# Attention and feed-forward stack: scores in two halves, products in two parts, and the variance by one full matmul

## The chip, the cores and the metric

The kernel runs on one core of one Trainium2 chip. The metric is the device time of one execution in microseconds (us), the median of several runs. The core has five engines that run side by side and meet only at semaphores: TensorE (PE: matmuls out of SBUF into PSUM), VectorE (DVE), ScalarE (ACT), GpSimd (POOL, which here touches SBUF alone) and SyncE (SP, which here issues the transfers).

## What is computed

The input is 2 batches of 1024 tokens of 128 features. The program is: norm and a first small attention, norm and a stack of six layers, norm and a second small attention, norm and the same stack again. Only the stack (`_L0_ffn_ref`) is touched. Cut to what matters, in fp32:

```python
for i in range(6):                        # 16 heads of 64, windows of 32
    x = attn_layer(shift_tokens(x), Wqkv[i], ...) + x
    x = ffn_layer(shift_tokens(x), ...) + x

def attn_layer(x, Wqkv, qs, ksc, Wo):
    q, k, v = split(x @ Wqkv)             # 128 -> 3 * 1024
    q, k = l2norm(q) * qs, l2norm(k) * ksc   # per head, then rotary tables
    out = local_attention(q, k, v)        # each window of 32 looks at itself and the one before
    return out @ Wo                       # 1024 -> 128

def ffn_layer(x, g, bln, W1, b1, W2, b2):
    mu = x.mean(-1); var = ((x - mu) ** 2).mean(-1)
    xn = (x - mu) / sqrt(var + 1e-05) * g + bln
    a, gate = split(xn @ W1 + b1)         # 128 -> 2 * 341
    return a * gelu(gate) @ W2 + b2
```

## The kernel before

`ffn_stack` is called twice, and each call runs 6 layers of 16 tiles of 128 tokens: 96 tiles. It is a software pipeline written out by hand. Each engine has a loop over the same slots `s`, 96 with a tile of their own (`live(s)`) and 13 more that drain. In slot `s` TensorE projects q, k and v of tile `s`, transposes the rotated and normalised q and k of tile `s-1` and forms its scores, forms the products of attention weights and v for tile `s-2` (`values`), and projects the output of tile `s-3` (`out_part`). The feed-forward part works on blocks of four tiles: `feed(s, lag)` names a block only in one slot of four. So slots come in four kinds by `s % 4`, called phase 0 to 3 here:

- phase 3: `feed(s, 7)` centres a block (L1140), squares and averages it, and `feed(s, 11)` does the third piece of the hidden half;
- phase 0: `feed(s, 8)` spreads the inverse deviation (L1145) and scales, and `feed(s, 12)` does the three matmuls with W2 (L1166, L1177, L1190);
- phase 1: `feed(s, 9)`, three gate matmuls (L1117); phase 2: `feed(s, 10)`, two hidden matmuls (L1117).

The order on an engine is the order of its instructions; nothing is scheduled elsewhere. TensorE's order in a slot is: q projection (L1077), q and k transposes (L1213, L1219), k projection, mask and scores (L1085, L1094), v projection, and then four parts of `values` (L1107, 32 matmuls each; an fp32 matmul leaves two records in the trace, so a part shows as 64) with `feed_first`, `feed_second` and `feed_third` between them, `feed_fourth`, and `out_part` (L1131). In phases 2 and 3 the first half of `out_part` stands between the third and the fourth part of `values`. Scores and products use small pieces of the array (64 rows by 32 columns, and 32 rows by 64), the others all of it.

Before `feed_first` TensorE waits for the evacuation of v (L1293 on ACT), since v's PSUM banks 6 and 7 are used again. Before the q projection of the next slot it waits for `o_ev`, the evacuation of the products (L1311 on ACT), which leave banks 0 to 3. Between one slot's projections and the next slot's transposes lies a chain over the other engines: ACT squares q (L1264), DVE rotates q and k (L1401 to L1404), takes the row maximum of the scores (L1440, which needs all scores), subtracts it (L1443), sums the squares (L1410, L1449), ACT takes logarithm and exponential (L1305, L1307), and POOL makes a Newton step (L1351 to L1357) and multiplies q, then k (L1361).

For the variance, TensorE takes each of four tiles of `xsq` as the stationary operand against one column `mean_of` (L1184), DVE adds epsilon (L1465), ACT makes a seed (L1317, L1319), POOL makes four small Newton operations (L1371 to L1377, 128x4), and TensorE spreads the result over the partitions (L1145), which DVE multiplies in (L1472) and POOL shifts (L1380).

## Time and profile before

| | us |
|---|---|
| median of 3 runs (4534.43 to 4556.44) | 4546.21 |
| the profiled execution, its own time | 4545.58 |
| its span, first to last instruction | 4543.7 |
| PE busy / DVE busy | 4139.5 / 3252.4 |
| ACT busy / POOL busy | 2299.8 / 2320.7 |
| mean granted TensorE clock | 0.964 of full speed |

The span is one execution on the chip. The two stacks fill it from about 420 to 2210 us and from about 2710 us to the end. A busy engine counts the durations of its instructions; a TensorE record's duration contains its pipeline's tail, so that records overlap and what counts for TensorE is the distance from one start to the next.

### The profile page before, as it was taken

The numbers are of one execution on the slowest core, as the hardware profiler recorded it, in microseconds if no ns is written. First come the engines' busy times: TensorE is split into PE (matmuls) and PEld (weight loads), VectorE is DVE, ScalarE is ACT, GpSimd is POOL, SyncE is SP. The second block draws the span as 40 slices with busy tenths as digits, with TensorE's granted clock in tenths as the row PEclk, the third lists the DMA queues.
The fourth block names the chain that finished last, engine by engine and source line by source line (L and its number), as shares of the span: only waits on it lengthen the run. The fifth ranks groups of instructions, "written<-read, shape, count | busy, mean of one in ns | idle before, by whom it ended". The sixth has DMA issues, their size and how long they took to land. (4 is left out here: it accounts for less than half of the span.)

```text
span 4543.7 us, 196701 instructions
## 1 busy us (share of the span) xinstructions
PE 4139.5 (91%) x90200; PEld 2525.9 (56%) x90200; DVE 3252.4 (72%) x4377; ACT 2299.8 (51%) x3044; POOL 2320.7 (51%) x2036
## 2 busy tenths in 40 slices
PE   6886899999999999999678877999999999999997
PEld 2322566666666666666333324666666666666664
DVE  7996677777777777777354435677777777777774
ACT  6884445555454555545224443455545455554553
POOL 0001567666666766766100005676676666666662
PEclk8998899999999999999789988999999999999998
DMA  0001111111211111111000001111111111121110
GB/s 19 1 1 40 44 51 39 52 40 45 55 31 54 46 41 53 37 31 31 12 1 1 1 12 55 51 42 50 46 42 52 37 54 46 35 60 37 31 35 20
DMA packets 92032, 162.95 MB, mean 36 GB/s; under 512 B 33996, under 2 KB 55240, under 8 KB 91208
## 3 DMA queue, kind: packets, MB, share of 16 engines
q1 hardware_dynamic: 91208, 150.36, 12.2%
q8 instruction: 712, 11.67, 1.1%
q14 instruction: 112, 0.92, 0.1%
HBM read 48.61 MB, written 1.05 MB: 11 GB/s over the span
## 5 line engine op out<-in xcount | busy, mean ns | idle before, releaser
L1107 PEld LDWEIGHTS banks<-f_P_T,f_V_previous 32*64 32x64 f32 x24576 | 482.6, 131 | 500.8 <-issue 479.9
L1349 POOL TENSOR_TENSOR f_q_rotated<-f_rope_aq,f_rope_bq 128x1024 f32<-128x1024 f32 x192 | 455.7, 2373 | 334.9 <-DVE f_rope_bq L1404 334.3
L1077 PE MATMUL banks<-f_wqkv,H 128*128 128x512 f32 x1152 | 574.5, 623 | 45.3 <-DMA f_wqkv<-in_L_ffn_Wqkv 21.2
L1107 PE MATMUL banks<-f_P_T,f_V 32*64 32x32 f32 x24576 | 577.9, 223 | 34.8 <-issue 33.6
L1401 DVE TENSOR_TENSOR f_rope_aq<-banks,f_rope 128x1024 f32<-128x1024 f32 x192 | 235.1, 1225 | 495.3 <-ACT f_sqq L1264 451.4
L1107 PE MATMUL banks<-f_P_T,f_V_previous 32*64 32x32 f32 x24576 | 569.0, 227 | 21.0 <-issue 13.7
L1349 POOL TENSOR_TENSOR f_k_rotated<-f_rope_ak,f_rope_bk 128x1024 f32<-128x1024 f32 x192 | 451.5, 2352 | 213.4 <-DVE f_rope_bk L1404 213.4
L1077 PE MATMUL banks<-f_wqkv,G 128*128 128x512 f32 x1152 | 554.0, 603 | 0.6
L1107 PEld LDWEIGHTS banks<-f_P_T,f_V 32*64 32x64 f32 x24576 | 441.3, 133 | 39.5 <-issue 38.4
L1336 POOL MEMSET f_kT<- 128x256 f32 x2 | 0.6, 311 | 847.6 <-POOLq L215 847.6
L1131 PE MATMUL banks<-f_O_T,f_wo 128*128 128x128 f32 x3072 | 429.7, 289 | 2.2 <-issue 2.1
L1264 ACT ACTIVATE f_sqq<-banks 128x1024 f32<-128x1024 f32 x192 | 197.0, 1026 | 439.4 <-PE banks L1077 439.4
L1131 PEld LDWEIGHTS banks<-f_O_T,f_wo 128*128 128x128 f32 x3072 | 382.9, 197 | 34.1 <-issue 26.0
L1293 ACT ACTIVATE f_V<-banks 128x1024 f32<-128x1024 f32 x192 | 196.5, 1023 | 401.5 <-PE banks L1077 401.5
L1311 ACT ACTIVATE f_O_T<-banks 128x1024 f32<-128x1024 f32 x192 | 196.5, 1023 | 363.1 <-PE banks L1107 363.0
L1361 POOL TENSOR_TENSOR f_q_rotated<-f_q_rotated,f_inverse_norm 128x1024 f32<-128x1024 f32 x192 | 365.1, 1902 | 15.1
L1367 POOL TENSOR_TENSOR f_E<-f_E,f_row_inverse 128x1024 f32<-128x1024 f32 x192 | 365.4, 1903 | 12.9 <-DVE f_row_inverse L1455 12.9
L1361 POOL TENSOR_TENSOR f_k_rotated<-f_k_rotated,f_inverse_norm 128x1024 f32<-128x1024 f32 x192 | 365.0, 1901 | 0.0
L1117 PE MATMUL banks<-f_xn,f_w 128*128 128x512 f32 (+1 forms) x576 | 322.8, 645 | 33.0 <-ACT f_V L1293 20.7
L1351 POOL TENSOR_TENSOR f_rsqrt_tmp<-f_rsqrt_seed 128x32 f32<-128x32 f32 x192 | 45.7, 238 | 553.3 <-ACT f_rsqrt_seed L1307 553.3
L1077 PEld LDWEIGHTS banks<-f_wqkv,H 128*128 128x128 f32 x1152 | 204.4, 198 | 210.4 <-issue 194.9
L1094 PEld LDWEIGHTS banks<-f_kT,f_qT 64*32 64x32 f32 x24576 | 253.9, 105 | 84.2 <-issue 81.7
(174 smaller groups left out, 8379.8 us busy)
## 6 DMA issues: line engine op xcount, KB each, us to landing
f_V_previous<-f_V SPq DMA_DIRECT2D x192, 384.0 KB, 3.7
f_V_previous<-f_V SPq DMA_DIRECT2D x192, 128.0 KB, 2.3
f_wqkv<-in_L_ffn_Wqkv SPq DMA_DIRECT2D x48, 384.0 KB, 4.0
f_rope<-in_rope SPq DMA_DIRECT2D x24, 512.0 KB, 5.2
f_wo<-in_L_ffn_Wo SPq DMA_DIRECT2D x12, 512.0 KB, 5.4
f_w<-in_L_ffn_W SPq DMA_DIRECT2D x12, 341.0 KB
f_w<-in_L_ffn_W SPq DMA_DIRECT2D x24, 64.0 KB
xin<-in_L_attn_a_x SPq DMA_DIRECT2D x2, 512.0 KB, 5.0
```

Of the source, the lines that this page charges most:

```text
L1077: mm = nc.tensor.matmul(ps[:, o * BLK:(o + 1) * BLK], xs, w[:, c * INNER + o * BLK:c * INNER + (o + 1) * BLK], start=True, stop=True)
L1094: mm = nc.tensor.matmul(PT_S[g * W:(g + 1) * W, c:c + 2 * W], qT[rows, k, g * W:(g + 1) * W], kT[u][rows, k, g * W:(g + 2) * W], start=Fal ...
L1107: mm = nc.tensor.matmul(banks[i * DH:(i + 1) * DH, g * BLK + k * W:g * BLK + (k + 1) * W], of[n % 3][r, h * DH:(h + 1) * DH], PT[n % 2][r, ...
L1117: nc.tensor.matmul(banks[0:k, bk * BLK:(bk + 1) * BLK], w1[b // NBLK % 2][:, half * DI + o:half * DI + o + k], xn[:], start=True, stop=Tru ...
L1131: mm = nc.tensor.matmul(bank(4, P), wo[layer(s - 3) % 2][:, k, :], OT[(n - 3) % 2][:, :, k, :], start=k == 0, stop=k == HP - 1)
L1264: nc.scalar.activation(sq[i][:], ps, ACT.Square).then_inc(sqd.sem, 1)
L1293: nc.scalar.activation(V[n % 3][:], PV_F, ACT.Copy).then_inc(v_ev.sem, 1)
L1311: nc.scalar.activation(OT[n % 2][:].rearrange("p g k t -> p g (k t)"), banks[:, 0:4 * BLK].rearrange("p (g c) -> p g c", g=NG)[:, :, 0:HP ...
L1349: nc.gpsimd.tensor_tensor(qk[i][:], ra[i][:], rb[i][:], ALU.add).then_inc(radd.sem, 1)
L1361: nc.gpsimd.tensor_tensor(heads_of(qk[i][:]), heads_of(qk[i][:]), over(rn[:, i * HEADS:(i + 1) * HEADS], DH), ALU.mult)\
L1367: nc.gpsimd.tensor_tensor(e, e, over(ri[:], DH), ALU.mult).then_inc(pn.sem, 1)
L1401: nc.vector.tensor_tensor(heads_of(ra[i][:]), src, table(2 * i, 0, DH), ALU.mult).then_inc(rot.sem, 1)
```

## The change

- `scores` is called in two halves of 4 head pairs each. The first half of the v projection stands between them, the second half behind them.
- `values` has two parts, of four head pairs (64 matmuls) each, and `out_part` is always whole and last. `feed_first` and `feed_second` stand together between the two parts; the first W2 matmul moves to `feed_first` and the second to `feed_second`.
- The variance is one matmul with a 128x128 stationary operand of 1/128 and `xsq` of 512 columns as the moving one. Its result is the variance of every token already spread over all partitions. So the four matmuls that spread it (L1145) go, and the steps on DVE, ACT and POOL that made it from 128x4 are 128x512 now. They use `xsq` as their temporary, and `rstd` stands in `var`.

```diff
-                    scores(n - 1, (s - 1) % TPB)
+                    scores(n - 1, (s - 1) % TPB, 0, HP // 2)
                 if live(s):
                     pe.wait_ge(kT_ev.sem, kT_ev.past(n - 1))
-                    project(s, 2, PV_F).then_inc(v_mm.sem, 1)
+                    project(s, 2, PV_F, 0, 1)
+                if live(s - 1):
+                    scores(n - 1, (s - 1) % TPB, HP // 2, HP)
+                if live(s):
+                    project(s, 2, PV_F, 1, 2).then_inc(v_mm.sem, 1)
...
-                    values(n - 2, 0, 2)
+                    values(n - 2, 0, 4)
...
                 feed_first(s)
-                if live(s - 2):
-                    values(n - 2, 2, 4)
                 feed_second(s)
                 if live(s - 2):
-                    values(n - 2, 4, 6)
+                    values(n - 2, 4, 8)
                 feed_third(s)
-                if live(s - 3) and s % TB >= 2:
-                    out_part(s, 0, HP // 2)
-                if live(s - 2):
-                    values(n - 2, 6, 8)
                 feed_fourth(s)
                 if live(s - 3):
-                    out_part(s, HP // 2 if s % TB >= 2 else 0, HP)
+                    out_part(s, 0, HP)
...
-                if (b := feed(s, 8)) is not None:
-                    pe.wait_ge(f_nt.sem, f_nt.at(blk(b)))
-                    for t in range(TB):
-                        mm = nc.tensor.matmul(banks[:, 6 * BLK + t * P:6 * BLK + (t + 1) * P],
-                                              rstd[:, t:t + 1].to_broadcast([P, P]), ident[:], start=True, stop=True)
-                    mm.then_inc(f_bc.sem, 1)
...
-                    for t in range(TB):
-                        mm = nc.tensor.matmul(banks[:, 5 * BLK + t:5 * BLK + t + 1], xsq[:, t * P:(t + 1) * P],
-                                              mean_of[:], start=True, stop=True)
-                    mm.then_inc(f_var.sem, 1)
+                    nc.tensor.matmul(bank(5), mean_of[:], xsq[:], start=True, stop=True).then_inc(f_var.sem, 1)
...
-                    nc.scalar.activation(vlg[:], var[:], ACT.Ln).then_inc(f_seed.sem, 1)
+                    nc.scalar.activation(xsq[:], var[:], ACT.Ln).then_inc(f_seed.sem, 1)
...
-                    nc.gpsimd.tensor_tensor(vrt[:], vy0[:], vy0[:], ALU.mult).then_inc(f_nt.sem, 1)
+                    nc.gpsimd.tensor_tensor(xsq[:], vy0[:], vy0[:], ALU.mult).then_inc(f_nt.sem, 1)
...
-                    nc.gpsimd.tensor_tensor(rstd[:], vrt[:], vy0[:], ALU.mult).then_inc(f_nt.sem, 1)
+                    nc.gpsimd.tensor_tensor(var[:], xsq[:], vy0[:], ALU.mult).then_inc(f_nt.sem, 1)
...
-                    nc.vector.scalar_tensor_tensor(xn[:], xcs[:], vec[b // NBLK % 2][:, 0:1], bank(6), ALU.mult, ALU.mult)\
+                    nc.vector.scalar_tensor_tensor(xn[:], xcs[:], vec[b // NBLK % 2][:, 0:1], var[:], ALU.mult, ALU.mult)\
```

How this moves TensorE's instructions, in the middle of a slot (`x64` counts matmuls of the program). Before, the scores stand in one piece and the v projection behind them:

```order
L1085 MATMUL banks<-f_band_mask,ident 128x512 x2
L1094 MATMUL banks<-f_kT,f_qT 32x64 x64
L1077 MATMUL banks<-f_wqkv,G 128x512 x2
L1107 MATMUL banks<-f_P_T,f_V_previous 64x32 x8
```

The same place of the changed kernel, where L1081, L1090, L1072 and L1104 are mask, scores, projection and products:

```order
L1081 MATMUL banks<-f_band_mask,ident 128x512 x2
L1090 MATMUL banks<-f_kT,f_qT 32x64 x32
L1072 MATMUL banks<-f_wqkv,G 128x512
L1090 MATMUL banks<-f_kT,f_qT 32x64 x32
L1072 MATMUL banks<-f_wqkv,G 128x512
L1104 MATMUL banks<-f_P_T,f_V_previous 64x32 x8
```

TensorE enters small pieces twice there now, with one matmul of the v projection between. The second place is the end of a phase 3 slot. Before, part three of the products, half the output projection, part four, the variance and the rest:

```order
L1107 MATMUL banks<-f_P_T,f_V 64x32 x8
L1131 MATMUL banks<-f_O_T,f_wo 128x128 x4
L1107 MATMUL banks<-f_P_T,f_V_previous 64x32 x8
L1107 MATMUL banks<-f_P_T,f_V 64x32 x8
L1107 MATMUL banks<-f_P_T,f_V_previous 64x32 x8
L1107 MATMUL banks<-f_P_T,f_V 64x32 x8
L1184 MATMUL banks<-f_mean_of,f_x_squared 128x1 x4
L1131 MATMUL banks<-f_O_T,f_wo 128x128 x4
L1077 MATMUL banks<-f_wqkv,G 128x512 x2
```

And the changed kernel from the second part's end on (L1174 is the variance, L1128 the output projection):

```order
L1104 MATMUL banks<-f_P_T,f_V 64x32 x8
L1174 MATMUL banks<-f_x_squared,f_mean_of 128x512
L1128 MATMUL banks<-f_O_T,f_wo 128x128 x8
L1072 MATMUL banks<-f_wqkv,G 128x512 x2
```

The output projection is in one piece and stands wholly behind the products. The third place is POOL, between the last multiplication of phase 3 (L1367) and the additions for the next tile (L1349), before:

```order
L1367 TENSOR_TENSOR f_E<-f_E,f_row_inverse 128x1024
L1371 TENSOR_TENSOR f_var_tmp<-f_var_seed 128x4
L1373 TENSOR_TENSOR f_var_tmp<-f_var_tmp,f_var 128x4
L1375 TENSOR_SCALAR f_var_tmp<-f_var_tmp 128x4
L1377 TENSOR_TENSOR f_rstd<-f_var_tmp,f_var_seed 128x4
L1349 TENSOR_TENSOR f_q_rotated<-f_rope_aq,f_rope_bq 128x1024
```

and in the changed kernel:

```order
L1354 TENSOR_TENSOR f_E<-f_E,f_row_inverse 128x1024
L1357 TENSOR_TENSOR f_x_squared<-f_var_seed 128x512
L1359 TENSOR_TENSOR f_x_squared<-f_x_squared,f_var_then_rstd 128x512
L1361 TENSOR_SCALAR f_x_squared<-f_x_squared 128x512
L1363 TENSOR_TENSOR f_var_then_rstd<-f_x_squared,f_var_seed 128x512
L1336 TENSOR_TENSOR f_q_rotated<-f_rope_aq,f_rope_bq 128x1024
```

The order there is the same; the four operations are 128 times as wide.

## Rows read from the trace of the kernel before

**Rows 1.** The page: the span, and TensorE's busy time.

```profile
span 4543.7 us, 196701 instructions
...
PE 4139.5 (91%) x90200; PEld 2525.9 (56%) x90200; DVE 3252.4 (72%) x4377; ACT 2299.8 (51%) x3044; POOL 2320.7 (51%) x2036
```

**Rows 2.** Windows, by engine: busy us (instructions), then PEclk, DMA share, GB/s.

```profile
1005.00:1010.00 5.00, 5.00 (x27) 3.70 (x27) 0.93 (x4) 1.43 (x3) 5.00 (x3) 0.66 0.40 108
...
1400.00:1800.00 400.00, 389.76 (x9827) 254.82 (x9824) 307.28 (x401) 210.75 (x276) 262.69 (x232) 1.00 0.18 48
```

**Rows 3.** Timeline of PE, a phase 2 slot: start, us, instruction, records, [idle before].

```profile
1045.87 1.88 PE L1077 MATMUL banks<-f_wqkv,H 128*128 128x512 f32 x4
...
1048.46 1.04 PE L1219 MATMUL banks<-ident,f_k_rotated 128*128 128x128 f32 x8
...
1051.58 1.48 PE L1094 MATMUL banks<-f_kT,f_qT 64*32 64x64 f32 x128
1052.99 1.98 PE L1077 MATMUL banks<-f_wqkv,H 128*128 128x512 f32 x4
1054.93 0.32 PE L1107 MATMUL banks<-f_P_T,f_V_previous 32*64 32x32 f32 x13
...
1056.09 1.12 PE L1117 MATMUL banks<-f_xn,f_w 128*128 128x512 f32 x2 [0.31 <-ACT f_V L1293]
1057.15 0.34 PE L1107 MATMUL banks<-f_P_T,f_V_previous 32*64 32x32 f32 x16
...
1057.94 1.12 PE L1117 MATMUL banks<-f_xn,f_w 128*128 128x512 f32 x2
...
1062.84 1.98 PE L1077 MATMUL banks<-f_wqkv,H 128*128 128x512 f32 x4
```

**Rows 4.** Timeline of PE, the three slots behind it (phases 3, 0, 1).

```profile
1065.54 1.04 PE L1219 MATMUL banks<-ident,f_k_rotated 128*128 128x128 f32 x8
...
1080.62 1.88 PE L1077 MATMUL banks<-f_wqkv,H 128*128 128x512 f32 x4
...
1096.41 1.12 PE L1190 MATMUL banks<-f_gate,f_w 85*128 85x512 f32 x2
1097.37 1.95 PE L1131 MATMUL banks<-f_O_T,f_wo 128*128 128x128 f32 x16
1099.16 1.88 PE L1077 MATMUL banks<-f_wqkv,H 128*128 128x512 f32 x4
...
1116.77 0.59 PE L1077 MATMUL banks<-f_wqkv,H 128*128 128x512 f32 x1
```

**Rows 5.** Timeline of DVE, ACT and POOL, same slots.

```profile
1054.75 1.22 DVE L1440 TENSOR_REDUCE f_row_max<-banks 128x16 f32<-128x1024 f32 x1
1055.02 1.02 ACT L1293 ACTIVATE f_V<-banks 128x1024 f32<-128x1024 f32 x1
...
1063.43 1.90 POOL L1361 TENSOR_TENSOR f_k_rotated<-f_k_rotated,f_inverse_norm 128x1024 f32<-128x1024 f32 x1
```

**Rows 6.** Groups of instructions: xcount, then busy us, mean ns, idle before.

```profile
L1349 POOL TENSOR_TENSOR f_q_rotated<-f_rope_aq,f_rope_bq 128x1024 f32<-128x1024 f32 x192 | 455.7, 2373 | 334.9 <-DVE f_rope_bq L1404 334.3 <-PE banks L1213 0.6
...
L1332 POOL TENSOR_TENSOR f_rope<-f_rope,f_qk_scales 128x512 f32<-128x512 f32 x48 | 59.6, 1273 | 20.7 <-DMA f_qk_scales<-in_L_ffn_k_scale 20.7
...
L1380 POOL TENSOR_SCALAR f_xn<-f_xn,f_ln_g_ln_b_b 128x512 f32<-128x512 f32 x48 | 33.3, 693 | 4.3 <-DVE f_xn L1472 4.3
...
L1298 ACT ACTIVATE f_x_squared<-banks 128x512 f32<-128x512 f32 x48 | 28.7, 597 | 59.9 <-PE banks L1140 59.9
```

**Rows 7.** Timeline of POOL and DVE around the phase 0 slot.

```profile
1084.23 0.20 POOL L1371 TENSOR_TENSOR f_var_tmp<-f_var_seed 128x4 f32<-128x4 f32 x1
...
1095.04 0.24 POOL L1351 TENSOR_TENSOR f_rsqrt_tmp<-f_rsqrt_seed 128x32 f32<-128x32 f32 x1 [3.02 <-ACT f_rsqrt_seed L1307]
...
1095.77 0.69 DVE L1472 SCALAR_TENSOR_TENSOR f_xn<-f_x_centered,f_ln_g_ln_b_b,banks 128x512 f32<-128x512 f32 x1
```

**Rows 8.** Timeline of POOL in the first stack's drain.

```profile
2201.39 0.20 POOL L1371 TENSOR_TENSOR f_var_tmp<-f_var_seed 128x4 f32<-128x4 f32 x1 [27.57 <-ACT f_var_seed L1319]
```

More of the change, by code:

```diff
@@ L1071, in banks67_free, with project @@
                     pe.wait_ge(h_new.sem, h_new.at(blk(b)))
-            def project(s, c, ps):
+            def project(s, c, ps, o0=0, o1=2):
                 xs = state(s)[:, col(s):col(s) + P]
                 w = wqkv[layer(s) % 2]
-                for o in range(2):
+                for o in range(o0, o1):
                     mm = nc.tensor.matmul(ps[:, o * BLK:(o + 1) * BLK], xs,
@@ L1079, in project, with scores @@
                 return mm
-            def scores(n, t):
+            def scores(n, t, k0, k1):
                 u = n % 2
-                pe.wait_ge(qT_ev.sem, qT_ev.at(n))
-                for i in range(2):
-                    nc.tensor.matmul(PT_S[:, i * BLK:(i + 1) * BLK], ident16[:],
-                                     mask[:, (1 if t else 0):(2 if t else 1), :].to_broadcast([P, HP, 2 * W]),
-                                     start=True, stop=False)
-                pe.wait_ge(kT_ev.sem, kT_ev.at(n))
-                for k in range(HP):
+                if k0 == 0:
+                    pe.wait_ge(qT_ev.sem, qT_ev.at(n))
+                    for i in range(2):
+                        nc.tensor.matmul(PT_S[:, i * BLK:(i + 1) * BLK], ident16[:],
+                                         mask[:, (1 if t else 0):(2 if t else 1), :].to_broadcast([P, HP, 2 * W]),
+                                         start=True, stop=False)
+                    pe.wait_ge(kT_ev.sem, kT_ev.at(n))
+                for k in range(k0, k1):
                     for i in range(2):
@@ L1096, in scores @@
                                 kT[u][rows, k, g * W:(g + 2) * W], start=False, stop=k == HP - 1)
-                mm.then_inc(s_mm.sem, 1)
+                if k1 == HP:
+                    mm.then_inc(s_mm.sem, 1)
             def values(n, k0, k1):
@@ L1141, in feed_first @@
                                      start=True, stop=True).then_inc(f_xc.sem, 1)
-                if (b := feed(s, 8)) is not None:
-                    pe.wait_ge(f_nt.sem, f_nt.at(blk(b)))
-                    for t in range(TB):
-                        mm = nc.tensor.matmul(banks[:, 6 * BLK + t * P:6 * BLK + (t + 1) * P],
-                                              rstd[:, t:t + 1].to_broadcast([P, P]), ident[:], start=True, stop=True)
-                    mm.then_inc(f_bc.sem, 1)
                 if (b := feed(s, 9)) is not None:
@@ L1154, in feed_first @@
                     hidden(b, 0, 0, 6, f_a.sem)
+                if (b := feed(s, 12)) is not None:
+                    pe.wait_ge(f_hm.sem, f_hm.at(blk(b), 2))
+                    nc.tensor.matmul(bank(7), w2[b // NBLK % 2][:, 0, :], ge[:, 0, :], start=True, stop=False)
             def feed_second(s):
@@ L1164, in feed_second @@
                 if (b := feed(s, 12)) is not None:
-                    pe.wait_ge(f_hm.sem, f_hm.at(blk(b), 2))
-                    nc.tensor.matmul(bank(7), w2[b // NBLK % 2][:, 0, :], ge[:, 0, :], start=True, stop=False)
+                    nc.tensor.matmul(bank(7), w2[b // NBLK % 2][:, 1, :], ge[:, 1, :], start=False, stop=False)
             def feed_third(s):
@@ L1175, in feed_third @@
                     hidden(b, 1, 2, 5, f_g.sem)
-                if (b := feed(s, 12)) is not None:
-                    nc.tensor.matmul(bank(7), w2[b // NBLK % 2][:, 1, :], ge[:, 1, :], start=False, stop=False)
             def feed_fourth(s):
@@ L1297, in _ @@
                     act.wait_ge(f_xc.sem, f_xc.at(blk(b)))
+                    act.wait_ge(f_nt.sem, f_nt.past(blk(b) - 1))
                     nc.scalar.activation(xsq[:], bank(6), ACT.Square).then_inc(f_sq.sem, 1)
@@ L1316, in _ @@
                     act.wait_ge(f_nt.sem, f_nt.past(blk(b) - 1))
-                    nc.scalar.activation(vlg[:], var[:], ACT.Ln).then_inc(f_seed.sem, 1)
+                    nc.scalar.activation(xsq[:], var[:], ACT.Ln).then_inc(f_seed.sem, 1)
                     act.wait_ge(f_seed.sem, f_seed.at(blk(b), 1))
-                    nc.scalar.activation(vy0[:], vlg[:], ACT.Exp, scale=-0.5).then_inc(f_seed.sem, 1)
+                    nc.scalar.activation(vy0[:], xsq[:], ACT.Exp, scale=-0.5).then_inc(f_seed.sem, 1)
                 if (b := feed(s, 9)) is not None:
@@ L1464, in _ @@
                     dve.wait_ge(f_nt.sem, f_nt.past(blk(b) - 1))
-                    nc.vector.tensor_scalar(var[:], bank(5, TB), EPS, None, ALU.add).then_inc(f_eps.sem, 1)
+                    nc.vector.tensor_scalar(var[:], bank(5), EPS, None, ALU.add).then_inc(f_eps.sem, 1)
                 if (b := feed(s, 8)) is not None:
```

19 lines of the change are left out of this document (7 added, 12 removed).

## Prediction

> **What bounds the kernel now.** I read the page first: TensorE is busy for 4139.5 of 4543.7 us, DVE, the next, for 3252.4 [rows 1]. Then the windows: from 1400 to 1800 us TensorE has work in 389.76 of 400 us, at the full granted clock, while DVE rests for nearly a quarter [rows 2]. So in the steady stack the length of a slot is the sum of TensorE's distances from start to start, and the timeline gives it. The q projections of five slots start at 1045.87, 1062.84, 1080.62, 1099.16 and 1116.77 [rows 3, 4]: phases 2, 3, 0 and 1 take 16.97, 17.78, 18.54 and 17.61 us, 70.90 for four slots. I call such four a period. All five stand in one place where nothing else disturbed TensorE.
>
> The reader should see one thing inside a slot. Small pieces are cheap and going in and out of them is dear. 128 score records take 1051.58 to 1052.99, 1.41 us; 64 product records take 1057.15 to 1057.94, 0.79 us [rows 3]. Half the records cost more than half the time: 64 more records cost 0.62, and 0.17 us is paid once a stretch. On the other side, two full records between two small parts take 1056.09 to 1057.15, 1.06 us, while a further record of a projection costs only 0.43 (four last 1.88 and one 0.59 [rows 4], so 1.29 for three), 0.86 for two. A stretch of small pieces thus costs 0.17 + 0.20 = 0.37 us beside its records. Second: the first part of the products, 1054.93 to 1056.09, takes 1.16 instead of 0.79, and the row names why: an idle 0.31, ended by the evacuation of v (1055.02 + 1.02 = 1056.04 [rows 5]).
>
> The second limit is near. k is multiplied on POOL until 1063.43 + 1.90 = 1065.33 [rows 5], and its transposes start at 1065.54 [rows 4]: 0.21 us of room, or 0.16 when 0.05 goes for a handoff (1056.04 to 1056.09 above). From one slot's k transposes, 1048.46 [rows 3], the chain over ACT, DVE and POOL needs until 1065.38, 16.92 us. No slot in which that chain is unchanged can be shorter than 16.92.
>
> **The change part by part**, TensorE first, from a slot's q projection.
>
> Up to the scores nothing changes: 1045.87 to 1051.58, 5.71 us. Scores and v projection took 1051.58 to 1054.93, 3.35. They are now two stretches of 64 records with two full records behind each: 0.79 + 1.06 + 0.79 + 1.06 = 3.70, so 0.35 is added in each slot. Products begin at 9.41.
>
> The first part of the products has 128 records, 0.79 + 0.62 = 1.41, taken as 1.44 with 0.01 a record. v's evacuation takes the same 1.16 from the end of the projection as before and is covered now: 0.37 us of waiting goes, and 0.28 of room is left. The feeds then stand together, four full records in phases 0 to 3: 1.06 + 0.86 = 1.92, until 12.77. The first and second W2 matmul are moved into this place in phase 0; both wait for gated values made two slots before, and nothing waits there. The second part is 1.44, until 14.21.
>
> Behind it phases 3, 0 and 1 have two full records (variance, third W2 matmul, third gate matmul) and the 16 of the output projection. The rows have just that: 1096.41 to 1097.37 to 1099.16, 0.96 + 1.79 = 2.75 [rows 4]. These slots end at 16.96. Phase 2 has the output projection alone, 1.79 + 0.10 for entering from small pieces: 16.10. The variance matmul is in these sums. It costs 0.96 in place of eight narrow records, so little moves there; the four spreading matmuls of phase 0 are simply gone.
>
> TensorE's own sum is 3 x 16.96 + 16.10 = 66.98. But 16.10 is under the chain's 16.92, so TensorE will wait some 0.82 us for k at the start of phase 3. The period is 3 x 16.96 + 16.92 = 67.80, which is 3.10 less than 70.90.
>
> Now what the chain sees. Its one new partner on TensorE is the row maximum, which needs all scores: they end at 5.71 + 2.64 = 8.35, and DVE gets to them at 1054.75 - 1045.87 = 8.88 [rows 3, 5]. So there is 0.4 of room and the later scores are free; without that room each 0.1 us would cost 0.1 in all 176 slots with feeds, 18 us. The earlier o_ev is free too: the products leave banks 0 to 3 1.8 us before the q projection, more than ACT's 1.02.
>
> Wider steps: epsilon on DVE and Ln and Exp on ACT go from 0.2 to about 0.6 us each (597 ns for 128x512 on ACT [rows 6]). They stand at the end of phase 3, behind the output's evacuation and ahead of the next squares. DVE is free for epsilon near 16.4, by its work before, and three steps of 0.6 with handoffs end near 18.4; queued behind them on ACT are the squares of the next q, wanted at 16.96 + 1.9 = 18.9. So 0.5 of room hides them.
>
> POOL's Newton step is the large one. 128x512 costs 1273 ns for a tensor_tensor and 693 for a tensor_scalar [rows 6]: 3 x 1.27 + 0.69 + three handoffs of 0.08 = 4.75 us in place of 1.1. No row shows these very operations; the bounds are nothing more than that line at one end and, at the other, the 2373 ns of an operation twice as wide, 8.05 us in all. I take the 1.27, the same width and form. Before, it started 3.61 us into phase 0 (1084.23 - 1080.62); phase 3 ahead of it is 0.82 shorter now and POOL's work is not, so it starts at 4.4 and ends at 9.2. Queued behind it are the two additions of some 2.37 us each: they end at 13.95. POOL's next need is the seeds at 1095.04 - 1080.62 = 14.42 [rows 7]. So 0.45 us of room is left and the step costs nothing while it is there. Without it, each us beyond costs 44 us over the run.
>
> The scaling L1472 reads the deviation from SBUF now, so both its tensors lie there. The row shows 0.69 us at 1095.77 with one of the two from PSUM, at the time of POOL's small Newton operations [rows 7]; no row has two from SBUF beside POOL. Between no cost and the whole 0.69 put in front of POOL's multiplications I take none for the sum. The Trainium skill speaks against that: "SBUF — State Buffer", the section on the separate sides of SBUF, says that a DVE operation with two SBUF inputs and a GpSimd operation take a shared pair of ports as an exclusive lock, and that the loser waits for the whole instruction. By it the sum would be that of the second rival below.
>
> Sum: 96 tiles a call less the first 8 slots, which have no feeds yet, make 22 periods, 44 in two calls: 44 x 3.10 = 136 us. The drain pays for the wider chain, since there everything waits for it: POOL idled 27.57 us before the last Newton step [rows 8]. 3.65 on POOL, 0.8 on ACT, 0.4 on DVE, less 1.1 for the spreading: 3.8 a call, 8 in two. The first 8 slots are bound by the chain and I leave them. 136 - 8 = 128, and 4545.58 - 128 = 4418. The profiled execution stands 0.6 us from the median of the runs, so this is the forecast for both.
>
> **The rivals.**
>
> *TensorE's sum alone* (chance 0.06): k comes earlier than I read, the period is 66.98, 44 x 3.92 = 172, less 8: 4382. Against it stands the 1065.33, which no part of the change moves.
>
> *DVE and POOL hinder each other at the scaling* (0.22). It starts at 15.15 in phase 0, amid small Newton operations that end at 15.6. If POOL's next steps wait some 0.55 us for it, k is ready at 17.47, not 16.92, and the slot is 0.5 longer: 44 x 0.5 = 22, so 4440. If instead DVE waits for both of POOL's multiplications, its additions to the state come 3.7 us late and the next q transposes stall for some 1.7 us: 75 us, so 4493. For it, only what the skill says in the place named above; against it, POOL's even durations, which no such operation ever met. The first form is the likelier.
>
> *POOL's Newton step overruns* (0.06). At 8.05 us it ends 3.3 later, 2.85 past its room; the slot becomes 19.8: 44 x 2.8 = 123, so 4541. A third of that gives 4460. Against: the 1273 ns are a mean of 48 with the same width.
>
> *The clock falls* (0.09), the one that ends on the other side. At 1005 to 1010 the granted clock was 0.66: of these 5 us 0.34 x 2 x 5 = 3.4 ran at 1.2 GHz in place of 2.4, which lost 1.7 [rows 2]. The changed kernel has, in every slot, small scores, two full records and 128 small products, 3.3 us with only 0.86 us of full records, and the wait of 0.8 in phase 3. If that lets the clock fall, each such stretch costs 1.7 us; 75 of them, one in 2.3 slots, cancel the 128, and one in each slot gives 4418 + 176 x 1.7 = 4717. The gain also removes causes: the wait for v and the narrow records. Against it: 1400 to 1800 at full clock with parts much like these.
>
> **How the numbers follow.** Forecast 0.57, its own range 4400 to 4436; the rivals 0.06, 0.22, 0.06, 0.09 as above. About 0.5%, 23 us, is what a measurement of this kernel can tell from no change. Faster by more: all but the worst of the overrun and the half of the clock's case that costs over 100 us, 0.90. The clock's case holds 0.05 for slower and most of the rest is the same. The range 4380 to 4490 takes TensorE's sum alone, both usual forms of the hindrance and a mild overrun: 0.83.
>
> **What would show it.** The period of q projections at 67.8; TensorE idle about 0.8 us before the k transposes in phase 3 alone, released by POOL; no idle before the first feed; 1.41 to 1.44 for 128 product records and 1.06 for half a v projection; POOL's three wide products at 1.27 us and its additions done before the seeds. Wrong would be: waits before the row maximum, k transposes waiting in phase 1 (hindrance) or before phase 1 by over 1 us (overrun), a mean clock under 0.96.

## The result: 0.36% faster, and the profile after

| | us |
|---|---|
| before, median of 20 runs (4534.43 to 4556.44) | 4544.64 |
| changed, median of 20 runs (4515.93 to 4548.97) | 4528.38 |
| ratio, with its 95% interval | 0.9964 (0.9955 to 0.9974) |
| the profiled execution of the changed kernel, its own time | 4523.63 |

The gain is 16 us where 128 were forecast. It is real, but inside the 0.5% that the prediction called no change, and outside its range. The page, which answers to [rows 1], shows that the span fell by 22 us in this execution, and TensorE's busy time by 85:

```profile
span 4521.8 us, 195415 instructions
...
PE 4054.1 (90%) x89528; PEld 2431.3 (54%) x89528; DVE 3279.5 (73%) x4377; ACT 2343.3 (52%) x3044; POOL 2495.5 (55%) x2036
...
q8 instruction: 707, 11.58, 1.1%
```

TensorE was thus idle or slow for most of what it saved. Windows over the two stacks (busy us and instructions of PE, PE's loads, DVE, ACT and POOL, then the granted clock, DMA share, GB/s):

```profile
570.00:2150.00 1580.00, 1515.87 (x38406) 974.21 (x38409) 1227.56 (x1585) 845.57 (x1079) 1131.76 (x924) 0.98 0.16 44
2900.00:4400.00 1500.00, 1441.64 (x36584) 924.01 (x36582) 1172.56 (x1513) 807.20 (x1029) 1080.88 (x882) 0.99 0.16 44
```

The first stretch of the kernel before, for comparison:

```profile
570.00:2150.00 1580.00, 1542.23 (x38621) 1010.06 (x38613) 1211.46 (x1579) 824.81 (x1078) 1050.21 (x922) 1.00 0.16 44
```

Where TensorE idled stands in the waits of the whole execution (us in total, times, longest):

```profile
PE banks L1104 <- issue: 116.6, 148, 2.5
...
PE banks L1128 <- issue: 19.5, 18, 2.4
...
PE banks L1207 <- POOL f_k_rotated L1348: 13.1, 26, 0.8
```

L1104 are the products. "issue" says that nothing in the program held them: no semaphore, no tile. The kernel before had this row too, less than half as large, and a wait for v that is gone now:

```profile
PE banks L1107 <- issue: 47.3, 58, 2.2
...
PE banks L1117 <- ACT f_V L1293: 20.7, 71, 0.3
```

One slot of phase 3, the counterpart of [rows 4], shows the rest. It is the timeline of PE; rows of a run that alternate between the two V tiles are left out:

```profile
1060.33 1.06 PE L1207 MATMUL banks<-ident,f_k_rotated 128*128 128x128 f32 x8 [0.21 <-POOL f_k_rotated L1348]
1061.23 1.88 PE L1072 MATMUL banks<-f_wqkv,H 128*128 128x512 f32 x4
...
1063.47 0.86 PE L1090 MATMUL banks<-f_kT,f_qT 64*32 64x64 f32 x64
1064.26 1.12 PE L1072 MATMUL banks<-f_wqkv,H 128*128 128x512 f32 x2
1065.32 0.86 PE L1090 MATMUL banks<-f_kT,f_qT 64*32 64x64 f32 x64
1066.10 1.12 PE L1072 MATMUL banks<-f_wqkv,H 128*128 128x512 f32 x2
1067.16 0.34 PE L1104 MATMUL banks<-f_P_T,f_V_previous 32*64 32x32 f32 x16
...
1068.30 0.28 PE L1104 MATMUL banks<-f_P_T,f_V 32*64 32x32 f32 x5
1069.36 0.31 PE L1104 MATMUL banks<-f_P_T,f_V 32*64 32x32 f32 x7 [0.78 <-issue]
1069.60 1.13 PE L1137 MATMUL banks<-G,f_center 128*128 128x512 f32 x2
1070.57 1.02 PE L1114 MATMUL banks<-f_xn,f_w 128*85 128x512 f32 x2
1071.52 0.34 PE L1104 MATMUL banks<-f_P_T,f_V_previous 32*64 32x32 f32 x16
...
1072.67 0.59 PE L1104 MATMUL banks<-f_P_T,f_V 32*64 32x32 f32 x13
1073.19 1.12 PE L1174 MATMUL banks<-f_x_squared,f_mean_of 128*128 128x512 f32 x2
1074.15 1.95 PE L1128 MATMUL banks<-f_O_T,f_wo 128*128 128x128 f32 x16
1075.94 1.88 PE L1072 MATMUL banks<-f_wqkv,H 128*128 128x512 f32 x4
```

Read the starts against the prediction. Half scores 0.79, half v projection 1.06, again 0.78 and 1.06: 3.69, as forecast 3.70. The two feeds 1.92, as forecast. Variance and output projection 0.96 + 1.79, as forecast. But the first product run takes 1067.16 to 1069.60, 2.44 us in place of 1.44, and the second 1.67. In the first, five records start from 1068.30 on and the next at 1069.36, a microsecond later: TensorE halts within one and the same run. (The row's 0.78 is counted from the modelled end of the record ahead.) Of the 174 product runs between 570 and 2150 us the shortest takes 1.42, so the 1.44 is possible; the median is 1.66 and the mean 1.80. The same holds for whole slots: the shortest of phases 0 to 3 take 16.89, 16.85, 16.03 and 16.89 us, close to the forecast, but their means are 18.14, 18.05, 17.07 and 18.28.

What ends a halt? The DMA view of this stretch, 1063 to 1074 us in 40 slices of 0.275 us, shows a queue that the prediction never looked at:

```profile
GB/s 0 0 0 0 0 0 0 0 0 0 0 0 0 60 0 0 0 0 0 0 0 0 0 0 0 0 0 60 0 0 0 0 0 0 0 0 0 0 0 0
...
q8 instruction: 2, 0.03, 1.2%
```

### The profile page after: what moved, and what is told of

Same layout as the page of the kernel before. It is cut to its first block and busy times, and to the rows that moved or that the text cites. A ratio compares the mean times of both kernels' runs of the same rounds, so it can differ in the third digit from the quotient of the medians.

```text
span 4521.8 us, 195415 instructions
## 1 busy us (share of the span) xinstructions
PE 4054.1 (90%) x89528; PEld 2431.3 (54%) x89528; DVE 3279.5 (73%) x4377; ACT 2343.3 (52%) x3044; POOL 2495.5 (55%) x2036
## 3 DMA queue, kind: packets, MB, share of 16 engines
q8 instruction: 707, 11.58, 1.1%
## 5 line engine op out<-in xcount | busy, mean ns | idle before, releaser
L1104 PEld LDWEIGHTS banks<-f_P_T,f_V_previous 32*64 32x64 f32 x24576 | 485.8, 131 | 341.8 <-issue 340.4
L1072 PE MATMUL banks<-f_wqkv,H 128*128 128x512 f32 x1152 | 597.2, 629 | 44.6 <-DMA f_wqkv<-in_L_ffn_Wqkv 21.3
L1104 PE MATMUL banks<-f_P_T,f_V 32*64 32x32 f32 x24576 | 555.0, 225 | 73.2 <-issue 72.0
L1104 PE MATMUL banks<-f_P_T,f_V_previous 32*64 32x32 f32 x24576 | 548.2, 227 | 46.7 <-issue 44.6
L1072 PE MATMUL banks<-f_wqkv,G 128*128 128x512 f32 x1152 | 579.8, 612 | 0.0
L1104 PEld LDWEIGHTS banks<-f_P_T,f_V 32*64 32x64 f32 x24576 | 463.2, 132 | 82.2 <-issue 81.0
L1128 PEld LDWEIGHTS banks<-f_O_T,f_wo 128*128 128x128 f32 x3072 | 395.0, 203 | 97.0 <-issue 94.5
L1128 PE MATMUL banks<-f_O_T,f_wo 128*128 128x128 f32 x3072 | 409.2, 289 | 19.7 <-issue 19.5
L1090 PEld LDWEIGHTS banks<-f_kT,f_qT 64*32 64x32 f32 x24576 | 267.1, 105 | 227.2 <-issue 224.6
L1090 PE MATMUL banks<-f_kT,f_qT 64*32 64x64 f32 x24576 | 328.9, 224 | 1.5 <-ACT f_kT L1267 1.5
L1114 PE MATMUL banks<-f_xn,f_w 128*128 128x512 f32 (+1 forms) x576 | 304.8, 640 | 23.1 <-DVE H L1467 11.3
L817 DVE TENSOR_REDUCE soft_neg_max<-banks 128x3 f32<-128x1536 f32 (+11 forms) x219 | 176.5, 854 | 163.1 <-PE banks L710 111.5
```

The lines of the kernel that those rows point to most:

```text
L817: nc.vector.tensor_reduce(pm[r % 2][:, it, jc, h0:h1], strips(j, h0, h1, n), AX.X, ALU.max, negate=True).then_inc(maxed, 1)
L1072: mm = nc.tensor.matmul(ps[:, o * BLK:(o + 1) * BLK], xs, w[:, c * INNER + o * BLK:c * INNER + (o + 1) * BLK], start=True, stop=True)
L1090: mm = nc.tensor.matmul(PT_S[g * W:(g + 1) * W, c:c + 2 * W], qT[rows, k, g * W:(g + 1) * W], kT[u][rows, k, g * W:(g + 2) * W], start=Fal ...
L1104: mm = nc.tensor.matmul(banks[i * DH:(i + 1) * DH, g * BLK + k * W:g * BLK + (k + 1) * W], of[n % 3][r, h * DH:(h + 1) * DH], PT[n % 2][r, ...
L1114: nc.tensor.matmul(banks[0:k, bk * BLK:(bk + 1) * BLK], w1[b // NBLK % 2][:, half * DI + o:half * DI + o + k], xn[:], start=True, stop=Tru ...
L1128: mm = nc.tensor.matmul(bank(4, P), wo[layer(s - 3) % 2][:, k, :], OT[(n - 3) % 2][:, :, k, :], start=k == 0, stop=k == HP - 1)
```

## The experiments

Two theories stood at the start. *Supply*: TensorE's instructions don't come fast enough for this dense stretch, so what counts is how many stand in how many microseconds. *Run length*: long runs of small pieces are slow in themselves. All ratios are to the kernel before, run on the same chip, with 95% intervals. Differences in us between two other kernels are of medians taken on different chips, whose medians for the kernel before lie within 6 us. The diffs give the order of the calls in short, against the kernel that the text names. A feed is a call that may hold no matmul: `feed_third` has one in phase 1 alone.

**Scores whole.** The changed kernel with the scores and the v projection as before.

```diff
-scores(n - 1, (s - 1) % TPB, 0, HP // 2); project(s, 2, PV_F, 0, 1)
-scores(n - 1, (s - 1) % TPB, HP // 2, HP); project(s, 2, PV_F, 1, 2)
+scores(n - 1, (s - 1) % TPB, 0, HP); project(s, 2, PV_F)
```

> The changed kernel with the scores in one piece again (no part of the computation is left out). My theory (supply): TensorE's instructions come in blocks, and between the first score and the last product it can't have them faster than a block in some 3.5 us; the 0.37 us of the switch that goes is then given back as a longer halt inside the products: 4510 to 4535. Rival (run length): a long run of small records halts for a price of its own, so the 0.35 us a slot come off in full: 4528 - 176 x 0.35 = 4466, 4455 to 4480.

Measured: 4504.71, 0.9903 (0.9884 to 0.9921). 24 us less than the changed kernel, between the two theories and nearer to supply: 0.35 us a slot are 62 us by the distances, and over half of them were lost again. By the account below only 8 us of that are halts inside small runs, 10 are the clock and 16 other waits, most of them the wait for k, which was 13.1 us in the changed kernel:

```profile
PE banks L1207 <- POOL f_k_rotated L1344: 29.6, 58, 0.9
```

So the chain over the other engines took nearly as much of this gain as halts and clock did, and the run says little on which theory is right.

**Products in four parts.** The changed kernel with a feed call behind every 64 product records. Since `feed_third` has a matmul in phase 1 alone and the output projection stands last, the trace shows four parts there only; in phases 0, 2 and 3 the last two parts are one run of 128 records.

```diff
-values 0-4, feed_first, feed_second, values 4-8, feed_third, feed_fourth
+values 0-2, feed_first, values 2-4, feed_second, values 4-6, feed_third, values 6-8, feed_fourth
```

> The changed kernel with the products in four parts of 32 matmuls and the feeds between them, as before, but the output projection whole (no part of the computation is left out). By the distances, two switches of 0.37 us and the 0.37 of waiting for v come back: +1.11 us a slot, 195 us, if the halts inside the products stay. Both theories (supply, run length) say that most of these halts, some 0.9 us a slot, go: +0.2 us a slot, 4540 to 4590. A result above 4680 would say that the halts have nothing to do with either.

Measured: 4548.1, 1.0006 (0.9996 to 1.0016), where both theories had it. With the split scores, this order costs 20 us more than two parts: the halts at the products fall from 116.6 to 76.0 us, and the wait for v comes back.

**Fewer instructions.** The changed kernel with half of its score instructions, and full records in their place. It leaves out half of the scores, so its result is not that of the program.

```diff
 scores(n - 1, (s - 1) % TPB, 0, HP // 2)
 project(s, 2, PV_F, 0, 1)
-scores(n - 1, (s - 1) % TPB, HP // 2, HP)
+project(s, 2, PV_F, 0, 1)
 project(s, 2, PV_F, 1, 2)
```

> The changed kernel with the second half of the score matmuls left out and the first half of the v projection made twice in its place: the same time by the distances within 0.13 us a slot, but 124 instructions fewer ahead of the products, which are untouched. Supply: the halts inside the two long product runs mostly go and slots come down towards the chain's 16.9 us: 4400 to 4450. Run length: the runs are as long as before, the halts stay: 4500 to 4528.

Measured: 4470.94, 0.9838 (0.9817 to 0.986). By the distances a slot is nearly as long as in the changed kernel (16.64 against 16.69 us in the account below), and still 57 us go. That lies between the two expectations, 21 us from supply and 29 from run length. The halts at the products fall from 116.6 to 69.7 us with the product runs untouched, which a fixed price of a run does not give; the wait for k rises from 13.1 to 35.8, so the chain's floor takes a part of what supply had promised.

**One more full matmul.** The changed kernel with the second half of the v projection done twice.

```diff
+                    project(s, 2, PV_F, 1, 2)
                     project(s, 2, PV_F, 1, 2).then_inc(v_mm.sem, 1)
```

> The changed kernel with the second half of the v projection made twice (no part left out): one more full matmul, 0.86 us, with 4 instructions, ahead of the products. Supply: TensorE would have halted anyway, and the block arrives meanwhile; 0.1 to 0.4 us a slot are left: 4546 to 4600. Run length, or TensorE's work as the limit: 0.86 x 176 = 151 on top: 4679, 4650 to 4700.

Measured: 4553.74, 1.0016 (1.0002 to 1.0031). 151 us of work (0.86 in 176 slots) cost 25. This is what tells the theories apart. Waits and windows:

```profile
PE banks L1104 <- issue: 64.9, 90, 2.2
```

```profile
570.00:2150.00 1580.00, 1555.67 (x38471) 991.28 (x38469) 1224.73 (x1579) 839.49 (x1074) 1127.80 (x921) 1.00 0.16 44
```

The halts fell from 116.6 to 64.9 us with the same product runs, and the granted clock came back to 1.00. By the account below, of the 151 us 59 were taken out of halts, 33 out of the half clock and 31 out of other waits, the wait for k among them.

**The same on the kernel before.**

```diff
-                    project(s, 2, PV_F).then_inc(v_mm.sem, 1)
+                    project(s, 2, PV_F)
+                    project(s, 2, PV_F, 1, 2).then_inc(v_mm.sem, 1)
```

> The kernel before with the second half of the v projection made twice (no part left out): the same 0.86 us a slot that cost the changed kernel 25 us, 151 by the distances. Supply: before the change TensorE halts for only some 60 us in its 176 full slots, so most of it is paid here: 4542 + 90 to 130, 4630 to 4675. Rival (the extra matmul is cheap anywhere, so its small price on the changed kernel says nothing): below 4590.

Measured: 4651.53, 1.0234 (1.0219 to 1.0249): 108 us for the same matmul, as supply had it. Before, TensorE's work was mostly the bound; after the change it is mostly not.

**Small matmuls instead.** The changed kernel with two head pairs of the products done twice, 64 records and their loads.

```diff
+                    values(n - 2, 0, 2)
                     values(n - 2, 0, 4)
```

> The changed kernel with the first 32 product matmuls made twice (no part left out): 64 more small records, 0.65 us by their distances, and 128 more instructions ahead of a product run. Supply: 128 instructions are half a block, and a block takes 3.5 us at the least where instructions are short: between 1.3 and 1.75 us a slot, 4750 to 4830, and in any case above the 115 us that the records themselves add. Rival (TensorE's work plus a price for each long run): 0.65 x 176 = 115, so 4635 to 4655.

Measured: 4951.44, 1.0905 (1.0877 to 1.0934). By the distances these records cost 0.62 to 0.79 us a slot, less than the full matmul; they cost 423 us, 2.4 a slot, and more than supply had said. The waits, and the windows:

```profile
PE banks L1104 <- issue: 304.7, 227, 2.5
```

```profile
570.00:2150.00 1580.00, 1456.00 (x39470) 945.44 (x39469) 1101.71 (x1419) 755.27 (x969) 1019.24 (x832) 0.95 0.15 41
```

Halts cost more than their length here: the clock is at 0.95 in this stretch, so that a tenth of it ran at 1.2 in place of 2.4 GHz. 108 halts inside product runs end 2.29 to 2.73 us after a block's start (8 in 10), the same offset as in the changed kernel.

**Scores whole, and three or four parts.** Both are the changed kernel with the scores as before. Four parts are four in phase 1 alone again, and 64, 64 and 128 records in the other phases.

```diff
+scores whole; values 0-3, feed_first, values 3-6, feed_second, values 6-8, feed_third, feed_fourth
```

> The changed kernel with whole scores and the products in three parts of 48, 48 and 32 matmuls with one full matmul behind the first and behind the second. By the distances its period is 67.9 us, that of the changed kernel (67.8). If what matters is the sum of instructions between the first score and the last product (one block in 3.5 us), it halts as the changed kernel does: 4505 to 4530. If what matters is that a block's 256 instructions are not used up within the 2.5 us that the next needs to come, the parts of 48 with a full matmul between help: 4430 to 4480.

```diff
+scores whole; values 0-2, feed_first, values 2-4, feed_second, values 4-6, feed_third, values 6-8, feed_fourth
```

> The changed kernel with whole scores and the products in four parts of 32, so that only the variance, the whole output projection and the places of two W2 matmuls are left of the change. By the distances a period of 69.2, 1.4 us more than the changed kernel's, 4480; supply adds halts about like those before the change, 10 to 50 us: 4490 to 4530. Run length says the same.

Measured: 4547.41, 1.0013 (0.9998 to 1.0028), for three; 4510.26, 0.9935 (0.9915 to 0.9954), for four. Four parts are where both theories had them; three parts are outside both of their ranges, 17 us above the higher one. Two, three and four parts give 4505, 4547 and 4510, so neither short runs nor long ones are good as such. Three parts have the largest halts of them all beside the extra small ones:

```profile
PE banks L1104 <- issue: 175.1, 182, 2.3
```

**Variance only.** The kernel before with the new variance and the new places of the first two W2 matmuls; scores, product parts and output projection as before. Against the changed kernel:

```diff
-scores in two halves around half of the v projection
+scores whole, v projection whole
-values 0-4, feed_first, feed_second, values 4-8, feed_third, feed_fourth, out_part whole
+values 0-2, feed_first, values 2-4, feed_second, values 4-6, feed_third,
+first half of out_part (phases 2, 3), values 6-8, feed_fourth, rest of out_part
```

> The kernel before with the new variance and the first two W2 matmuls one place earlier, and nothing else. By the distances the spreading (1.09 us) and one switch (0.16) go in phase 0: 1.25 x 44 = 55 us, of which a halt in the one product run of 64 matmuls in four slots may take back up to 20: 4492 to 4515. If the wide Newton step or the hindrance of DVE and POOL cost time, the gain is below 20 us: above 4527.

Measured: 4498.62, 0.9902 (0.9887 to 0.9917): 43 us less than before, where both theories had it, and 30 less than the whole change. Waits and windows:

```profile
PE banks L1104 <- issue: 60.4, 70, 2.4
...
PE banks L1114 <- ACT f_V L1281: 22.1, 76, 0.4
```

```profile
570.00:2150.00 1580.00, 1534.60 (x38961) 987.49 (x38963) 1239.39 (x1599) 852.36 (x1090) 1145.80 (x935) 1.00 0.16 44
```

The wait for v is back, 22 us here and 11 and 10 at two other lines, and it costs less than the halts of the whole change.

**Two parts only, and scores split only.** The other two thirds of the change, each on the kernel before.

```diff
-values 0-2, feed_first, values 2-4, feed_second, values 4-6, feed_third,
-first half of out_part (phases 2, 3), values 6-8, feed_fourth, rest of out_part
+values 0-4, feed_first, feed_second, values 4-8, feed_third, feed_fourth, out_part whole
```

> The kernel before with the products in two parts and the output projection whole, and nothing else. By the distances slots at the chain's floor, a period of 67.9 in place of 70.9, 4542 - 132 = 4410. Supply: the dense stretch is 1.6 us shorter than before with the same instructions, so halts and half clock give most of it back, as with whole scores on the changed kernel (4505): 4495 to 4540.

```diff
-scores whole, v projection whole
+scores first half, half of v projection, scores second half, other half
```

> The kernel before with the scores in two halves around the halves of the v projection, and nothing else. By the distances +0.35 us a slot, 62 us: 4604. Supply: the 0.35 fall partly into halts that are there already, up to half: 4570 to 4604. If splitting spares a halt of its own (long score runs as the cause), it costs nothing: 4535 to 4555.

Measured: 4536.2, 0.9987 (0.9973 to 1.0001), and 4583.62, 1.0084 (1.0071 to 1.0097). Two parts alone gain nothing that can be measured: their halts at the products are 95.6 us in place of 47.3. Splitting the scores costs 40 us, less than the 62 of its distances, and its halts are 32.3 in place of 47.3, which fits that it brings more time for the same instructions. Both are where supply had them.

**W2 late.** Variance only, with the first two W2 matmuls back at the second and third feed.

> The kernel before with the new variance only, the W2 matmuls at their old places. In phase 0 the first two product parts are now one run and cover the wait for v, 0.37 us in four slots, 16 us less than variance_only by the distances: 4483. Supply: the run of 64 comes right behind scores and projection, where instructions are scarcest, and takes some of it back: 4480 to 4500. Both say that it beats the changed kernel.

Measured: 4524.15, 0.9954 (0.994 to 0.9968), outside both expectations. Its edit against the variance-only kernel:

```diff
-feed_first(s):  first W2 matmul;   feed_second(s): second W2 matmul
+feed_second(s): first W2 matmul;   feed_third(s):  second W2 matmul
```

Both kernels have one run of 128 product records in phase 0. In the variance-only kernel it is the last one, and here the first, right behind the scores and the projection. The forecast that it would cover the wait for v was wrong from the start, since that wait stands in the program between the first part and `feed_first`, and so inside this run:

```profile
PE banks L1104 <- ACT f_V L1281: 11.8, 42, 0.3
```

The medians are 26 us apart. In the profiled executions, 21 us apart, the slots of phase 0 are 0.31 us longer in the mean (18.27 against 17.96), some 14 us in 44 of them; the next part of 64 records halts there in 25 of 42 slots. So the place of a run counts, with no work added.

**Sums.** From the start records of TensorE I made this account of the 176 slots with feeds and products (slots 8 to 95 of each call). A halt is a distance above the usual one of its pair of records by over 0.06 us; half of the time at half clock counts as lost; the rest is divided by 176. Two things make the rest too small where much runs at half clock: small records hardly slow down there (product records start 13.0 ns apart in place of 11), and a halt inside such a stretch is counted in both columns. With the additional small matmuls some 47 us of halts lie so, and their rest is only 0.37 us a slot above the changed kernel's, where the records take at least 0.62.

| kernel | 176 slots, us | lost to the half clock | halts inside small runs | other halts and waits | rest, us a slot |
|---|---|---|---|---|---|
| before | 3158 | 5 | 50 | 57 | 17.30 |
| changed | 3149 | 40 | 129 | 44 | 16.69 |
| scores whole | 3126 | 50 | 137 | 60 | 16.36 |
| products in four | 3162 | 5 | 66 | 81 | 17.10 |
| whole and three | 3180 | 33 | 200 | 14 | 16.67 |
| whole and four | 3129 | 17 | 82 | 79 | 16.77 |
| one more full matmul | 3171 | 7 | 70 | 13 | 17.51 |
| small matmuls | 3532 | 178 | 324 | 27 | 17.06 |
| fewer instructions | 3084 | 28 | 66 | 62 | 16.64 |
| variance only | 3121 | 12 | 59 | 60 | 16.99 |

The same halts, run by run, show where they fall. The table gives the sum of the distances above 0.07 us inside a run, less the usual 0.01 of each, over the 42 to 44 slots of one phase (slots 9 to 94 of each call):

| small run | kernels | us lost in one phase |
|---|---|---|
| 128 scores | before, scores whole, variance only | 0 to 3 |
| 64 products, second to fourth part | before | 1 to 9 |
| 96 products, first part | whole and three | 4 to 7 |
| 96 products, second part | whole and three | 31 to 32 |
| 128 products | changed, both parts | 13 to 17 |
| 128 products, last part | products in four, whole and four, variance only | 15 to 18 |
| 128 products | one more full matmul, both parts | 2 to 12 |
| 192 products, first part | small matmuls | 63 to 70 |

A run of 128 products loses nearly the same wherever it is the last part, which speaks for run length. But 128 scores, with full-size matmuls ahead, lose almost nothing, 96 products in second place lose twice what 128 lose, and the same 128 lose less with one full matmul more ahead. So a fixed price of a run's length is ruled out, and what stands ahead of it counts.

## Why the prediction failed, step by step

**The step that failed** is the price of a long product run: "64 more records cost 0.62", and with it "the first part of the products has 128 records, 0.79 + 0.62 = 1.41, taken as 1.44", and the same for the second part. The 0.62 was the difference between a run of 128 score records and one of 64 product records [rows 3]. The shortest product run takes 1.42 us, so the array can keep that price. It was read where 5.7 us with few instructions, projections and transposes, stand ahead. Behind the scores, and twice, it is not kept: the median is 1.66 and the mean 1.80. Below it lies a wrong premise, "in the steady stack the length of a slot is the sum of TensorE's distances": a sum of distances can be shortened beyond what instructions arrive for. Even before the change the premise did not hold to the full: the period of 70.90 us was read in an undisturbed place, and the mean of this execution is 71.9.

**What became of the 128 us.** The rest a slot fell by 0.61 us, 107 us over 176 slots, and other waits by 13 (v's is gone, k's has come). These 120 answer to the 136 forecast for the slots. Halts inside small runs took back 79 and the half clock 35. That leaves 3158 - 3149 = 9 us; rounding of the table is in it. The profiled spans differ by 22 and the medians by 16.

**The clock** was a rival, and it came in part: 40 us are lost at 1.2 GHz where it was 5. The prediction looked for its cause in the small pieces; the runs show it with the halts. One more full matmul, with as many small pieces, brings it to 7, and small matmuls with 324 us of halts to 178. The trace shows the order within a kernel too. The longest stretch at half clock of the changed kernel's first stack begins at 1443.3 us, in a halt, and the full matmuls behind it take 2.08 us where they took 1.12:

```profile
1443.71 0.46 PE L1104 MATMUL banks<-f_P_T,f_V 32*64 32x32 f32 x12 [1.88 <-issue]
1444.10 2.08 PE L1148 MATMUL banks<-f_gate,f_w 128*128 128x512 f32 x2
```

Between 570 and 2150 us the clock falls 10 times in the changed kernel, and 7 times a halt in a product run stands just ahead (I looked 4 us back); with the small matmuls it is 32 of 33. That the halts are the cause is argued from this, since no run changes the halts and nothing else.

**What held.** The split scores cost 0.34 a slot by the distances, and by themselves 40 us in the whole, where the 0.35 gave 62. The wait for v left. The wait for k came in phase 3, released by POOL as forecast, but smaller than the 0.82 us: 19 of the 44 slots have none, the transposes of k start 0.17 us late in the median and 1.0 at most. Halts lengthen the slot ahead of it, while the chain stays as it was. POOL's Newton step hides: in the phase 0 slot below, POOL is through with its additions 1.64 us before the seeds come (the idle time in the first row), and 1.07 us at least in all 44 such slots, where 0.45 was forecast. These are its groups (busy us, mean ns, idle before), which answer to the estimate from [rows 6]:

```profile
L1359 POOL TENSOR_TENSOR f_x_squared<-f_x_squared,f_var_then_rstd 128x512 f32<-128x512 f32 x48 | 61.3, 1277 | 3.8
L1363 POOL TENSOR_TENSOR f_var_then_rstd<-f_x_squared,f_var_seed 128x512 f32<-128x512 f32 x48 | 61.2, 1274 | 4.0
...
L1357 POOL TENSOR_TENSOR f_x_squared<-f_var_seed 128x512 f32<-128x512 f32 x48 | 49.9, 1039 | 45.7 <-ACT f_var_seed L1306 45.7
...
L1361 POOL TENSOR_SCALAR f_x_squared<-f_x_squared 128x512 f32<-128x512 f32 x48 | 29.7, 618 | 4.2
```

1.27 twice as taken; the square, whose two inputs are one tensor, 1.04. That the full variance matmul is a good trade is shown by the variance-only kernel.

**The hindrance between DVE and POOL** came too, in each of the 44 slots of phase 0, and cost little. Timeline of POOL and DVE in a phase 0 slot, the place of [rows 7]:

```profile
1090.36 0.24 POOL L1338 TENSOR_TENSOR f_rsqrt_tmp<-f_rsqrt_seed 128x32 f32<-128x32 f32 x1 [1.64 <-ACT f_rsqrt_seed L1294]
...
1090.68 0.25 POOL L1340 TENSOR_TENSOR f_rsqrt_tmp<-f_rsqrt_tmp,f_sum_of_squares 128x32 f32<-128x32 f32 x1
...
1091.09 0.69 DVE L1458 SCALAR_TENSOR_TENSOR f_xn<-f_x_centered,f_ln_g_ln_b_b,f_var_then_rstd 128x512 f32<-128x512 f32 x1
...
1091.31 0.57 POOL L1344 TENSOR_TENSOR f_inverse_norm<-f_rsqrt_tmp,f_rsqrt_seed 128x32 f32<-128x32 f32 x1
```

The small operation of POOL lasts 0.57 us where its median is 0.252, and ends 0.10 after DVE's. Behind it stand the multiplications of q and k, and the chain is 0.32 us longer in this phase, 17.25 in place of 16.92. This trace agrees with what the Trainium skill, "SBUF — State Buffer", states of two SBUF inputs on DVE against GpSimd. The first form of the rival expected 22 us from it; phase 0 slots have some 0.4 us of room now in the median, since the halts make them longer. Where they don't, the sign that the prediction had named appears: the k transposes of phase 1 wait in 11 of 44 slots, 0.3 us at most and 2.2 us in all.

**What stays open.** That the supply is what halts TensorE rests on four things: "issue" as the only cause, the fixed offset behind a block, a full matmul that is nearly free where small ones cost three to four times what their distances say (109 to 139 us), and the same full matmul at 108 us on the kernel before. No run changes the supply itself and nothing else, so this stays an inference. How the halts depend on where a block's border falls in the slot is not settled: three parts at 4547 between two at 4505 and four at 4510 have nearly equal counts of instructions, and neither theory gave that; the halts of three parts sit in the second run of 96, but why just there is open. Blocks of other engines may be among those on q8; the count of records fits TensorE alone.

The three parts of the change, each by itself, gain 43 us (variance with the W2 places), gain 7 (two parts, within the uncertainty) and lose 40 (split scores): 10 together, near the 16 of the whole. The lowest medians are variance only, 4498.62, and scores whole, 4504.71, too close to be told apart here; both beat both kernels.

## What to carry to other kernels

A timeline's distances tell what the array can do, not what an instruction stream can feed it: where hundreds of small matmuls and loads follow each other, count instructions per microsecond and look at the queue that brings the program before pricing denser packing. Halts named "issue" that lie inside a run of one kind of matmul, with no releaser, are the sign that this limit is near, and the prediction never read them, although the kernel before had 47.3 us of them. When a change has several independent parts, price and run each alone: one part here was worth nearly three times the whole.

## What the runs showed of the hardware that was not expected

- The program comes in blocks of 16.38 KB, 254 TensorE records each, at least 3.3 us apart in 99 of 100 cases and 4.2 in the median (changed kernel, 570 to 2150 us); halted runs go on 2.3 to 2.7 us after a block's start.
- A full matmul of 0.86 us in each slot cost 108 us on the kernel before and 25 on the changed one; 64 small records, which take less by their distances, cost 423 there.
- Equal runs of small matmuls cost by their place: 96 product records lose 4 to 7 us over one phase's slots as the first part and 31 as the second.
- The granted clock goes with it: 0.961 of full speed over the whole execution for the changed kernel, 0.967 with the full matmul, 0.931 with the small ones.
- Going into small pieces and out again costs 0.37 us by the distances; doing that once more in each slot cost 40 us in all, 0.23 a slot.
